# A new order for the attention and feed-forward pipeline: 32-token blocks paired 0/2 and 1/3, one value copy, the feed-forward in another PSUM bank

## The reference

```
for i in range(DEPTH):                                   # 6
    x = attn_layer(shift_tokens(x), Wqkv[i], q_scale[i], k_scale[i], Wo[i]) + x
    x = ffn_layer(shift_tokens(x), ln_g[i], ln_b[i], W1[i], b1[i], W2[i], b2[i]) + x

def attn_layer(x, ...):                                  # 16 heads of 64, windows of 32 tokens
    q, k, v = split(x @ Wqkv)
    q, k = l2norm(q) * qs, l2norm(k) * ksc               # then rotary tables on both
    sim = q k^T * 8      # own window and the window before, masked
    out = softmax(sim) @ [v of the window before, v of the own window]
    return out @ Wo

def ffn_layer(x, ...):
    xn = layernorm(x) * g + bln
    a, gate = split(xn @ W1 + b1)                        # 341 hidden
    return a * gelu(gate) @ W2 + b2
```

## Time and profile before

| | |
|---|---|
| Median of 3 runs | 4047.65 us (4046.55 to 4050.84) |
| Profiled execution | 4048.09 us, its span 4046.3 us |
| PE busy over the span | 3729.9 us, 92% |
| DVE busy | 3487.8 us, 86% |
| ACT busy | 3422.3 us, 85% |
| POOL busy | 2387.8 us, 59% |
| Granted TensorE clock | 0.982 in the mean |
| PE busy 1000 to 3500 us | 2351.87 us of 2500, granted clock 1.00 |

### The profile page before, as it was taken

The page is one execution under the profiler, slowest core; times in us unless marked ns, Lnnn a source line. Parts: engine busy times, 40 slices in busy tenths (PEclk is TensorE's granted clock), DMA queues, the critical chain, the costliest instruction groups (busy, mean ns, idle before and its releaser), DMA issues.

```text
span 4046.3 us, 125302 instructions
## 1 busy us (share of the span) xinstructions
PE 3729.9 (92%) x49248; PEld 2338.2 (58%) x49248; DVE 3487.8 (86%) x7192; ACT 3422.3 (85%) x9269; POOL 2387.8 (59%) x1420
## 2 busy tenths in 40 slices
PE   5999999967999999999999999999999999998987
PEld 2444444434666666666666666666666666666665
DVE  6999999957889898888988888898898888888884
ACT  3999999956888888888888888888888888888885
POOL 2434443436666666666666666666666666666662
PEclk7999999988999999999999999999999999999998
DMA  1000001002333333333333333333343333433332
GB/s 50 8 9 9 9 9 36 1 0 50 80 76 77 90 85 81 75 80 86 87 82 74 80 77 95 85 77 77 76 98 80 79 76 75 98 82 79 76 82 56
DMA packets 158791, 263.19 MB, mean 65 GB/s; under 512 B 45696, under 2 KB 72064, under 8 KB 157952
## 3 DMA queue, kind: packets, MB, share of 16 engines
q1 hardware_dynamic: 158208, 255.20, 26.8%
HBM read 26.43 MB, written 2.10 MB: 7 GB/s over the span
## 4 chain that ended last, share of the span: by engine, by line
PE 62%; DVE 18%; ACT 12%; issue 3%; POOL 2%; SPq 1%; DMA 1%; DVEq 0%; POOLq 0%; ACTq 0%
PE ps L655 17%; ACT arena L931 6%; PE ps L601 5%; PE ps L596 5%; PE ps L688 5%; PE ps L724 5%; PE ps L542 4%; PE ps L733 4%; PE ps L762 3%; PE ps L709 3%; PE ps L768 3%; DVE ssq L1164 3%; PE ps L537 3%; PE ps L775 3%; DVE arena L1147 2%
## 5 line engine op out<-in xcount | busy, mean ns | idle before, releaser
L655 PE MATMUL ps<-WB,arena 128*128 128x512 f32 x2304 | 1110.5, 605 | 132.5 <-DVE arena L1244 61.4
L931 ACT ACTIVATE arena<-arena,nmx 128x64 f32<-128x64 f32 x3072 | 1020.1, 337 | 4.4 <-DVE arena L1222 3.8
L475 POOL TENSOR_TENSOR arena<-arena 128x1024 f32<-128x1024 f32 x192 | 454.4, 2367 | 516.3 <-DVE arena L1147 516.0
L655 PEld LDWEIGHTS ps<-WB,arena 128*128 128x128 f32 x2304 | 399.9, 192 | 463.2 <-issue 438.8
L907 ACT ACTIVATE arena<-ps 128x1024 f32<-128x1024 f32 x384 | 393.5, 1025 | 314.1 <-PE ps L655 307.7
L491 POOL TENSOR_TENSOR arena<-arena,rinv 128x1024 f32<-128x1024 f32 x192 | 365.2, 1902 | 389.9 <-DVE rinv L1195 389.9
L931 ACT ACTIVATION_READ_ACCUMULATOR arena<-arena,nmx 128x1 f32 x3072 | 584.3, 190 | 0.0
L1141 DVE TENSOR_TENSOR arena<-ps,tables 128x1024 f32<-128x1024 f32 x384 | 464.7, 1210 | 87.4 <-ACT arena L907 87.4
L688 PEld LDWEIGHTS ps<-ident,arena 128*128 128x128 f32 x3072 | 355.6, 141 | 239.1 <-issue 173.6
L1147 DVE TENSOR_TENSOR arena<-ps,tables 128x512 f32<-128x512 f32 x768 | 489.9, 678 | 0.0
L480 POOL TENSOR_TENSOR arena<-arena 128x1024 f32<-128x1024 f32 x192 | 455.1, 2371 | 30.8 <-DVE arena L1147 30.8
(11 more groups left out here) (109 smaller groups left out, 6675.9 us busy)
## 6 DMA issues: line engine op xcount, KB each, us to landing
arena<-arena SPq DMA_DIRECT2D x768, 128.0 KB, 2.3
arena<-arena SPq DMA_DIRECT2D x1536, 64.0 KB
WB<-wb SPq DMA_DIRECT2D x24, 512.0 KB, 5.0
arena<-X SPq DMA_DIRECT2D x384, 32.0 KB, 1.9
arena<-Y SPq DMA_DIRECT2D x96, 128.0 KB, 2.4
arena<-wa SPq DMA_DIRECT2D x8, 581.0 KB, 3.8
WF<-wf SPq DMA_DIRECT2D x6, 537.5 KB, 4.5
keep<-xT SPq DMA_DIRECT2D x1, 2048.0 KB, 7.8
```

Source lines behind the costliest of these rows:

```text
L475: pool.tensor_tensor(tu[:, K], t1[:, K], t2[:, K], ALU.add).then_inc(addk_r, 1)
L655: i = pe.matmul(banks[:, c, :], xs_[t % RING], WB[:, w * INNER + c * COL:w * INNER + (c + 1) * COL], start=True, stop=True)
L931: i = act.activation(pe3[:, :, h, :], sc[:, 64 * h:64 * h + 64].rearrange("p (k q) -> p k q", k=2), ACT.Exp, bias=nmx[:, h:h + 1], accum_o ...
```

## The change

Six things are done at once, all in the second stack.

1. The windows are paired 0/2 and 1/3 instead of 0/1 and 2/3. One side of the pair is then the tile's values as they are, so ACT copies them in one instruction of 128x1024 instead of two of 64x1024, and `vshift` needs 2 DMAs (96 rows and 32 rows) instead of 4 of 32 rows.
2. The feed-forward's turned inputs and its output go to bank 7 (`FO_BANK`), the second output bank, instead of banks 2 and 3, which the queries use. Their waits change with it (`o_free` for `q_free`).
3. `attend` moves from the end of a step to the second place of the next one.
4. The feed-forward runs one step later. The range of steps begins at -3.
5. On ACT the last four exponentials stand behind `values`, between the feed-forward's second and third gelu in a gate step. On DVE each rotation is split, sine first, with `turn_probs` and the statistics between the halves. POOL begins with `probs_norm`.
6. On SP the order of a step is now `ff_in`, `widen`, `vshift` (for s-1), `xs`; before, it was `xs`, `widen`, `ff_in`, `vshift` (for s).

```
-LAG = 12
+LAG = 14
-        FF_BANK = 2, 3
+        FF_BANK, FO_BANK = (2, 3), 7
@@ widen
-                    q, o = slice(WIN * w, WIN * (w + 1)), (WIN * w + 64) % P
-                    here = slice((w % 2) * COL, (w % 2 + 1) * COL)
+                    q, o = slice(WIN * w, WIN * (w + 1)), (WIN * w + 96) % P
+                    here = slice((w // 2) * COL, (w // 2 + 1) * COL)
...
@@ vshift
-                for dst, side, src, row, held in ((64, 0, (t - 1) % RING, 96, 1), (96, 0, r, 0, 0), (0, 1, r, 32, 0),
-                                                  (32, 1, r, 64, 1)):
-                    sp.dma_start(vv[r][dst:dst + WIN, side, :], vv[src][row:row + WIN, held, :])\
-                        .then_inc(vs_in, 16)
+                sp.dma_start(vv[r][0:96, 0, :], vv[r][0:96, 1, :]).then_inc(vs_in, 16)
+                sp.dma_start(vv[r][96:P, 0, :], vv[(t - 1) % RING][96:P, 1, :]).then_inc(vs_in, 16)
@@ SP's loop
-            for s in range(-2, TILES + LAG):
+            for s in range(-3, TILES + LAG):
+                if chunk(s, 6) is not None:
+                    ff_in(chunk(s, 6))
+                if live(s - 2):
+                    widen(s - 2)
+                if live(s - 1):
+                    vshift(s - 1)
                 if live(s + 2):
                     xs(s + 2)
-                if live(s - 2):
-                    widen(s - 2)
...
-                if chunk(s, 6) is not None:
-                    ff_in(chunk(s, 6))
-                if live(s):
-                    vshift(s)
@@ POOL's loop
+                if live(s - 2):
+                    probs_norm(s - 2)
+                if live(s):
+                    unit_q(s)
                 if live(s + 1):
                     add_k(s + 1)
+                if chunk(s, 8) is not None:
+                    ff_rstd(chunk(s, 8))
+                if live(s + 1):
                     add_q(s + 1)
                     unit_k(s + 1)
...
@@ PE
+            def o_free(s, lag):
+                need(pe, ot_r, min(s - lag + 1, TILES))
...
@@ ACT
-            def values(t, side):
...
+            def values(t):
+                act.wait_ge(v_mm, t + 1)
+                need(act, vs_in, 32 * (t - 1))
+                act.activation(vv[t % RING][:, 1, :], kv_ps.rearrange("p b c -> p (b c)"), ACT.Copy).then_inc(v_r, 1)
@@ DVE's loop
+                if live(s + 1):
+                    sin_k(s + 1)
                 if live(s - 2):
                     turn_probs(s - 2)
                 if live(s + 1):
-                    rotate_k(s + 1)
-                    rotate_q(s + 1)
+                    cos_k(s + 1)
+                    sin_q(s + 1)
+                if chunk(s, 8) is not None:
+                    ff_stats(chunk(s, 8))
+                if live(s + 1):
+                    cos_q(s + 1)
                 if live(s - 3):
                     residual(s - 3)
                 if live(s + 1):
                     sumsq(s + 1)
+                if chunk(s, 10) is not None:
+                    ff_hidden(chunk(s, 10), 0)
+                    ff_hidden(chunk(s, 10), 1)
+                if chunk(s, 8) is not None:
+                    ff_unit(chunk(s, 8))
+                if live(s + 1):
                     norms(s + 1)
...
```

More of the change, by code:

```diff
@@ L403, in _ @@
                     outputs_in((s - 2) // NT)
[L404 to L410 removed]
+                if 0 < (s - 8) // NT < LAYERS and (s - 8) % NT == 0:
+                    hidden_in((s - 8) // NT)
+                q = chunk(s, 12)
                 if q is not None and q >= FF - NT // PER:
@@ L669, in queries_of @@
                 first(t, lq)
-                need(pe, rotq_r, t)
-                for q, lag, count, each in ((chunk(t - 2, 7), 7, fn_r, 1), (chunk(t - 2, 8), 8, xn_r, 1),
-                                            (chunk(t - 2, 9), 9, hf_r, MF), (chunk(t - 2, 10), 10, fin_r, 1)):
-                    if q is not None:
-                        pe.wait_ge(count, each * (q + 1))
+                need(pe, rotq_r, 2 * t)
+                q = chunk(t - 2, 10)
+                if q is not None:
+                    pe.wait_ge(hf_r, MF * (q + 1))
                 product(t, 0, q_ps, q_mm)
@@ L715, in attend @@
                 pe.wait_ge(wide_in, 32 * PARTS * (t + 1))
-                pe.wait_ge(vs_in, 16 * PARTS * (t + 1))
+                pe.wait_ge(vs_in, 32 * (t + 1))
                 if t > 0:
                     hold(pe, y_r, t)
+                for q, count in ((chunk(t + 2, 8), fn_r), (chunk(t + 2, 9), xn_r), (chunk(t + 2, 11), fin_r)):
+                    if q is not None:
+                        pe.wait_ge(count, q + 1)
                 pw = PTd.rearrange("p (r s a c q) -> p r s a c q", r=2, s=2, a=2, c=NP)
@@ L772, in ff_down @@
                 pe.wait_ge(hf_r, MF * (q + 1))
-                q_free(s)
+                o_free(s, 3)
                 for m in range(MF):
-                    i = pe.matmul(ps[:, FF_BANK[0], :], WF[0:FW[m], F_W2 + m * D:F_W2 + (m + 1) * D], hf[m][0:FW[m], :],
+                    i = pe.matmul(ps[:, FO_BANK, :], WF[0:FW[m], F_W2 + m * D:F_W2 + (m + 1) * D], hf[m][0:FW[m], :],
                                   start=(m == 0), stop=(m == MF - 1))
                 i.then_inc(o_mm, 1)
-            for s in range(-2, TILES + LAG):
+            for s in range(-3, TILES + LAG):
                 if live(s + 1):
                     keys_of(s + 1)
-                if live(s):
-                    turn_k(s)
+                if live(s - 3):
+                    attend(s - 3)
                 if live(s + 1):
@@ L786, in _ @@
                 if live(s):
-                    turn_q(s)
+                    turn_k(s)
+                if chunk(s, 8) is not None:
+                    ff_turn(s, chunk(s, 8))
+                if chunk(s, 9) is not None:
+                    ff_back(s, chunk(s, 9))
                 if live(s - 3):
@@ L964, in _ @@
             keys_on(0)
-            for s in range(-2, TILES + LAG):
+            for s in range(-3, TILES + LAG):
                 if live(s + 1):
                     square(s + 1, kv_ps, K, k_mm, sqk_r)
-                if live(s):
-                    turned_k(s)
+                if live(s - 3):
+                    outputs(s - 3)
                 if live(s + 1):
```

151 lines of the change are left out of this document (64 added, 87 removed).

## The result

| | median, us | runs | ratio to before, 95% interval | granted clock |
|---|---|---|---|---|
| before | 4049.24 | 4046.55 to 4051.36 | | 0.982 |
| changed | 4556.18 | 4535.41 to 4562.53 | 1.1242 [1.1213, 1.1272] | 0.934 |
| forecast | 4210 | 4110 to 4300 | 1.040 | 1.00 in the middle |

The change costs 507 us, three times the forecast. The new tables, which DVE builds once per layer, mark its length: before, four layers take 3453.73 - 1413.75 us, 510.0 each; after, 3887.00 - 1501.75, 596.3 each. So a cycle of four steps went from 63.75 to 74.5 us, and six layers of +86.3 are 518 us: the loss is spread over the whole stack, and not made in single places.

A forecast was written before the change was run, and what follows sets the result against it. PE's own work, 94% busy, was taken as a floor nearby. 4048 us plus 144 over 48 chunks plus 26 at layer boundaries is 4218, less a little for unseen cover: 4210 us, range 4110 to 4300.

The forecast's parts named there:

- The ring: Loop from keys through square, sine, transpose, `widen`, `vshift` and input loads to the next keys: at least 14.7 us.
- Rivals 1 and 2: On SP's loads: SP keeps ahead, 3947 us, chance 0.11; only the gate step pays, about 4033 us, chance 0.06.
- Rival 3: On ACT, a table switch costs twice its row: down step 19.0 us instead of 15.1, about 4395 us; chance 0.03.
- the landing: Second load of tile s+2 on SP: lands 1.9 us after its issue, with an allowance of 0.3 added.
- PE's granted clock stays at 1.00: On PE: clock stays at the 2.4 GHz level, since PE would be busy for about 90% of a cycle.
- The upper bound: Slow landings near 3.5 us, or waits behind `vshift`: ring A + 10.0 after transpose end A, cycle about 69.5, 4360 us.
- The gate step's wait for the residual: SP's `ff_in` waits for this step's residual until 9.4 us, so the gate step takes 19.8 us instead of 18.21.
- The forecast's 66.5: Cycle of four steps, 15.2, 16.4, 19.8 and 15.1 us, against 63.5 before: +3.0 us per cycle.
- A + 8.9: From A, the end of DVE's transpose, through `widen`, `vshift` and the loads to their landing: 8.9 us, before the allowance.
- the boundary's 3.8: At each of five layer boundaries, key weights issued behind the tile's input land later: +3.8 us.
- The sum of the other parts: Cycle without the ring, 13.65, 14.1, 18.6 and 15.0 us by step: 61.4 us, 3947 us in all.

The follow-up runs named there:

- Experiment 1: Changed kernel with the two loads of tile s+2 (`xs`) first in SP's step again, ahead of `ff_in`, `widen` and `vshift`; 4059.11 us, ratio 1.0033.
- experiment 5: Changed kernel plus 24 unused transposes on PE ahead of each step's keys, except in the step after the down step; 4478.94 us, ratio 1.1068.
- experiment 2: Changed kernel with `ff_in` moved behind `xs` on SP; 4550.67 us, ratio 1.1249.
- experiment 11: Changed kernel with half of the score matmuls left out, so its output differs; one execution, 4469.27 us.

## Why the prediction was right in kind and wrong in size

**The ring was there, as described.** From the transpose to `widen`, `vshift`, `xs` and the next keys. Experiment 1 opens it and takes 497 us away. PE's largest wait, SP's waits for the transpose and the residual, and the missing wait for the value copy are the ones that were named. SP's longest, for `attend` (301.7 us), was not named, but the transpose comes after it. Rivals 1 and 2 fall with the waits in 39 of 53 steps. Rival 3 falls with the idle time of 0.8 us ahead of 55 table loads. Its sign, a down step that grew, did show (16.8 us, not its 19.0), but for another reason, as said below.

The Trainium skill, "ScalarE: Activation LUTs", section "What ACT_TABLE_LOAD costs", states a load of about 1283 ns and a drain of about 1380 ns for every switch. The 1283 ns show here, the drain does not.

**What failed.** Two steps of the prediction: the landing, "lands 1.9 us after its issue", and "PE's granted clock stays at 1.00". The ring in its parts, forecast and measured (medians, us):

| | turn-in | turn-back | gate | down |
|---|---|---|---|---|
| keys to first `widen` | 6.0, 6.13 | 7.2, 6.89 | 10.6, 12.50 | 5.5, 6.14 |
| `widen` to first `xs` | 6.2, 6.66 | 6.2, 6.36 | 6.2, 7.38 | 6.2, 6.36 |
| first `xs` to keys | 2.9, 4.62 | 2.9, 4.65 | 2.9, 3.17 | 2.9, 3.99 |

- *Landing, a term that was mis-sized.* It was put at 1.9, with an allowance of 0.3, from the median of loads that were issued ahead of everything. In the new place the load follows 512 KB of `vshift`, which makes 2.4 to 2.6 of it, and in turn-in and turn-back steps it meets an instruction transfer, which makes 3.5 and 3.8 of the second load. In sum that is +3.7 us of the 8.5 per cycle that were missing, over the three steps that end in a wait for it. The upper bound had been set by the slow end of the earlier trace rows, 3.5, but the range stopped short of it.
- *"PE's granted clock stays at 1.00."* Wrong, and not a matter of size: I took the clock from PE's mean busy share, while it falls behind single waits. The keys last 3.3 us in the median in turn-back steps, 3.6 in gate steps and 2.6 in down steps, and since squares and rotations come behind the keys, this is inside the ring. It is most of the gate step's +1.9 in the first row: the residual ends 11.3 us after the keys, instead of the 9.4 forecast, and at 9.6 in experiment 5, where the keys are fast. The down step shows it outside the ring. There 15.1 was forecast and 16.8 measured, with 0.1 us of idle time of PE in the whole step: the loads had landed before, and PE's own work took longer. In experiment 5 the step has 15.3. So the 3.99 of its last row is no landing, and its +1.7 is the clock. The clock is an amplifier: the longer ring makes the wait, the wait the slow keys, the slow keys a longer ring.
- *Issues.* One of the 0.59 us took 1.60 in the gate step, as the row at 2537.31 shows. +1.2 there, 0.2 to 0.5 elsewhere.
- *The gate step's wait for the residual* is where it was forecast, but experiment 2 shows that its cost can't be had back alone.
- *The sum itself.* The forecast's 66.5 adds typical steps and was set against 63.5, a mean; the typical steps of before add up to 63.04. That leaves out 0.5 x 48, some 22 us. Of the smaller sums, the ring's "A + 8.9" is 8.8 by its own terms and the boundary's 3.8 is 4.0, which changes nothing.

In all, 74.5 us per cycle instead of some 67.1 with its share of the boundaries is 7.4 x 48 = 355 us, which is close to the 346 between 4210 and 4556.

**What the ring hid.** The sum of the other parts, 61.4 us, has the right median (61.7) and was still 110 us off in the total (4059 and 3950): a cycle added up from its typical steps leaves out the boundaries, the stalls of PE and their slow keys. The kernel before has only small ones of these: its sum of 63.2 has a mean of 63.7, experiment 1's 61.7 one of 64.2. Another 22 us of the 110 are a slip of the sum itself, above. Why the stalls for PE's instructions are longer in the new order stays open: the transfers are as many (391 and 392).

## What to carry to other kernels

Before a transfer is moved behind others in a queue, follow the queue from the last thing that it waits for to the first thing that waits for the transfer; if both lie on the same cycle, the cycle's length is set by that sum and not by the engines. Take the landing time from transfers with the same traffic ahead of them, and keep its slow end in the range. Where a new wait of a few microseconds falls on PE in every step, read the clock of single microseconds behind such waits in the trace before, and price the next matmuls at half speed.

## What the runs showed of the hardware

- A 32 KB load landed in 1.9 us in the kernel before, in 2.4 to 2.6 us behind 512 KB of copies, and in up to 4.2 us with one 16 KB instruction transfer in flight.
- PE's instructions came over a queue of their own, 64 bytes each (24,576 fewer in experiment 11, 96 transfers of 16 KB fewer), and 19 stalls of PE in experiment 1, up to 3.3 us long, each ended 1.2 to 1.6 us after such a transfer.
- The granted clock fell from 1.00 to 0.50 behind single waits of PE of 2.6 to 4 us, and what came next ran at the lower level: the four matmuls of 1.95 us took 3.1 to 3.66. It did so behind most such waits and not behind all: in 5 of 14 down steps the keys still took 1.98 us, behind waits of 1.8 to 2.7.
- An issue on SP took 0.53 to 0.59 us for 64 KB and for 384 KB alike. The landing did differ with size: 1.9 us for 32 KB and 5.3 for 512 KB in the kernel before.
